# Expert tiles taken one at a time or two at a time on TensorE, in a convolution, attention and mixture-of-experts block

## The reference, cut to what matters

```python
def _L1_ffn_ref(x, router_w, w1, w2, w3):
    flat = x.reshape(-1, C)
    probs = softmax(flat @ router_w.T, axis=-1)
    topk_probs, topk_idx = jax.lax.top_k(probs, TOP_K)
    topk_probs = topk_probs / (sum(topk_probs) + 1e-09)
    gates = jnp.einsum('nk,nke->ne', topk_probs, onehot)
    h1 = jnp.einsum('nc,ehc->neh', flat, w1)
    h3 = jnp.einsum('nc,ehc->neh', flat, w3)
    h = jax.nn.silu(h1) * h3
    y = jnp.einsum('neh,ech->nec', h, w2)
    out = jnp.einsum('ne,nec->nc', gates, y)
```

## Time and profile before

| what | value |
|---|---|
| median of 3 runs | 802.6 us (799.39 to 805.01) |
| the profiled execution, its own time | 802.19 us |
| its span, first to last instruction | 800.4 us |
| mean granted TensorE clock | 0.851 of 2.4 GHz |
| TensorE matmul busy | 650.6 us, 81% of the span |
| the expert tiles, first ups to last scatter landed | 427.4 us to about 780.7 us |

### The profile page before, as it was taken

How to read it: one execution, slowest core, us unless ns; L and a number is a source line. 1 busy time by engine, 2 the same in 40 slices (tenths; PEclk the granted TensorE clock), 3 DMA queues, 4 the chain that set the end, 5 groups by cost and what they waited for, 6 DMA issues and landing times.

```text
span 800.4 us, 13968 instructions
## 1 busy us (share of the span) xinstructions
PE 650.6 (81%) x4632; PEld 487.2 (61%) x4632; DVE 463.2 (58%) x1094; ACT 353.7 (44%) x693; POOL 371.8 (46%) x377
## 2 busy tenths in 40 slices
PE   2597989797979797866206999999999999999960
PEld 2475858585857576664104777677777777777740
DVE  2356677686868676643502566655555665555545
ACT  1143646373727273533203555455555445555520
POOL 2204241767676768727670343334444333444440
PEclk9667868797978788575656999999999999999995
DMA  2000000010101010101173455555556455554608
GB/s 85 0 14 1 14 1 14 19 49 17 51 18 38 18 38 17 51 5 53 50 182 86 148 161 160 165 161 162 179 161 167 152 168 168 179 156 150 191 8 314
DMA packets 46615, 75.47 MB, mean 94 GB/s; under 512 B 7488, under 2 KB 30048, under 8 KB 46544
## 3 DMA queue, kind: packets, MB, share of 16 engines
q1 hardware_dynamic: 34512, 57.12, 24.5%
q0 software_dynamic: 8640, 12.74, 4.8%
q10 hardware_dynamic: 3392, 4.73, 1.8%
HBM read 58.54 MB, written 16.47 MB: 94 GB/s over the span
## 4 chain that ended last, share of the span: by engine, by line
PE 49%; POOL 23%; issue 17%; DVE 6%; DMA 3%; ACT 1%; POOLq 0%; SPq 0%; ACTq 0%; DVEq 0%
PE bk L757 25%; POOL expert_rows L497 15%; PE bk L768 12%; PE bk L745 3%; POOL rr L452 3%; PE bk L775 2%; POOL r L463 1%; PE bk L554 1%; POOL r L458 1%; POOL x2t L481 1%; DMA out<-hid 1%; DMA srow<-expert_results 1%; PE bk L642 1%; POOL grstd L441 1%; PE bk L616 1%
## 5 line engine op out<-in xcount | busy, mean ns | idle before, releaser
L1266 DVE TENSOR_TENSOR units<-bk,silu 128x512 f32<-128x512 f32 x213 | 147.3, 692 | 165.7 <-ACT silu L943 165.7
L519 POOL DMA_INDIRECT expert_results<-yout,xin x142 | 139.5, 983 | 218.3 <-DVE yout L1277 191.5
L757 PE MATMUL bk<-xs,wbuf 64*128 64x256 f32 x1704 | 205.5, 388 | 1.1 <-ACT xs L930 1.1
L757 PEld LDWEIGHTS bk<-xs,wbuf 64*128 64x128 f32 x1704 | 160.8, 189 | 44.4 <-issue 26.6
L943 ACT ACTIVATE silu<-bk 128x512 f32<-128x512 f32 x213 | 127.2, 597 | 87.2 <-PE bk L757 87.2
L497 POOL DMA_INDIRECT expert_rows<-srow,pos x128 | 132.4, 1034 | 44.2 <-issue 37.9
L768 PE MATMUL bk<-units,wbuf 128*64 128x256 f32 x852 | 107.6, 388 | 0.0
L768 PEld LDWEIGHTS bk<-units,wbuf 128*64 128x64 f32 x852 | 54.8, 136 | 32.4 <-issue 11.7
L935 ACT ACTIVATE ysb<-bk 128x256 f32<-128x256 f32 x71 | 27.2, 383 | 84.3 <-PE bk L768 84.3
L452 POOL TENSOR_TENSOR rr<-vare,c_mhalf 128x16 f32<-128x16 f32 x8 | 23.4, 2923 | 74.6 <-DVE vare L1046 74.6
L745 PE MATMUL bk<-const,xin 128*128 128x128 f32 x142 | 31.3, 302 | 29.2 <-DMA xin<-expert_rows 29.2
(11 more groups left out here) (184 smaller groups left out, 963.2 us busy)
## 6 DMA issues: line engine op xcount, KB each, us to landing
wbuf<-in_weights SPq DMA_DIRECT2D x71, 576.0 KB, 4.1
xin<-expert_rows SPq DMA_DIRECT2D x71, 130.0 KB, 2.4
expert_results<-yout,xin POOLq DMA_INDIRECT x142, 2.8
xg<-in_x SPq DMA_DIRECT2D x8, 256.0 KB, 2.8
expert_rows<-srow,pos POOLq DMA_INDIRECT x128, 2.4
srow<-expert_results SPq DMA_DIRECT2D x8, 256.0 KB, 5.1
srow<-expert_results ACTq DMA_DIRECT2D x8, 256.0 KB, 5.9
out<-hid ACTq DMA_DIRECT2D x8, 256.0 KB, 5.2
```

Source lines behind the costliest of these rows:

```text
L519: g.indirect_dma_start(results[:, :], bass.IndirectOffsetOnAxis(ap=xin[:, t % X_SLOTS, h, ROW - 1:ROW].bitcast(U32), axis=0), yout[:, t % ...
L757: last = mm(bank[:, ch * MT:(ch + 1) * MT], wbuf[part, t % W_SLOTS, at:at + P], xs[part, t % 2, :], start=True, stop=True)
L1266: tt(units[:, t % 2, q, :], h3_ps[q], silu[:, q, :], ALU.mult).then_inc(unit_ready, 1)
```

## The change

Tiles are taken in pairs (0, 1), (2, 3), ...; the last pair has one tile. On PE the order becomes: the six up groups of both tiles of pair i, the four row turns of pair i+1, the four result turns of pair i-1, then down of both tiles of pair i. To make this possible:

- `xs` holds two tiles side by side, and ACT stores the turned rows of both in one activation of 512 columns.
- The turned results of both tiles go to one bank, `turned_ps`, which is the bank `h3_ps[0]` of the ups; so result turns wait for the product of group 0 of the pair's second tile, and the next pair's ups wait until `gate_out` has read the bank (`yout_ready`).
- `down` of a tile now comes in the same round as its ups and not in the next.
- `gate_out` does a pair with three operations of 256 columns, and raises `yout_ready` once for both tiles.
- ACT stores the results of both tiles after the turned rows.
- POOL's loop is the same but waits for the pair's `yout_ready`. SP's program is unchanged.

```diff
-            for t in range(NT):
-                pool.wait_ge(yout_ready, t + 1)
+                pool.wait_ge(yout_ready, t // 2 + 1)
...
             def turn_rows(t):
                 pe.wait_ge(xin_loaded[t % X_SLOTS], 16 * (t // X_SLOTS + 1))
-                wait(pe, silu_ready, NU * (t - 1) + 1)
+                wait(pe, silu_ready, NU * (t - 1 - t % 2) + 1)
...
             def up(t, q):
                 if q == 0:
-                    pe.wait_ge(xs_ready, t + 1)
+                    pe.wait_ge(xs_ready, t // 2 + 1)
                     pe.wait_ge(w_loaded[t % W_SLOTS], 16 * (t // W_SLOTS + 1))
+                    wait(pe, yout_ready, t // 2 - 1)
                 wait(pe, unit_ready, NU * (t - 1) + q + 1)
...
             def down(t):
-                wait(pe, yout_ready, t - 1)
+                wait(pe, ysb_ready, t - 1)
                 pe.wait_ge(unit_ready, NU * (t + 1))
...
             def turn_results(t):
                 pe.wait_ge(ysb_ready, t + 1)
+                wait(pe, yout_ready, t // 2)
+                wait(pe, unit_ready, NU * min(2 * (t // 2) + 3, NT - 1) + 1)
                 for h in range(2):
-                    last = turn(yt_banks[t % 2][:, MT + h * P:MT + (h + 1) * P], ysb[:, t % 2, h * P:(h + 1) * P], ident)
+                    at = (2 * (t % 2) + h) * P
+                    last = turn(turned_ps[:, at:at + P], ysb[:, t % 2, h * P:(h + 1) * P], ident)
                 last.then_inc(y_turned, 1)
 
-            turn_rows(0)
-            for t in range(NT):
-                for q in range(NU):
-                    up(t, q)
-                if t + 1 < NT:
-                    turn_rows(t + 1)
-                if t > 1:
-                    turn_results(t - 2)
-                if t > 0:
-                    down(t - 1)
-            turn_results(NT - 2)
-            down(NT - 1)
-            turn_results(NT - 1)
+            for t in range(2):
+                turn_rows(t)
+            for i in range(NPAIR):
+                for t in pair(i):
+                    for q in range(NU):
+                        up(t, q)
+                if i + 1 < NPAIR:
+                    for t in pair(i + 1):
+                        turn_rows(t)
+                if i > 0:
+                    for t in pair(i - 1):
+                        turn_results(t)
+                for t in pair(i):
+                    down(t)
+            for t in pair(NPAIR - 1):
+                turn_results(t)
...
+            def store_xs(i):
+                n = len(pair(i))
+                act.wait_ge(xt_turned, 2 * i + n)
+                wait(act, h3_ready, NU * 2 * i)
+                f(xs[:, 0:n * MT], xt_ps[:, 0:n * MT], ACT.Copy).then_inc(xs_ready, 1)
...
+            def gate_out(i):
+                n = len(pair(i))
+                dve.wait_ge(y_turned, 2 * i + n)
...
+                v.tensor_copy(ysum[:, 0:n, :, :], halves[:, :, :, 0, :]).then_inc(ysum_ready, 1)
+                dve.wait_ge(ysum_ready, 2 * i + 1)
+                tt(ysum[:, 0:n, :, :], halves[:, :, :, 1, :], ysum[:, 0:n, :, :], ALU.add).then_inc(ysum_ready, 1)
+                dve.wait_ge(ysum_ready, 2 * i + 2)
+                tt(yout[:, at:at + n, :, :], ysum[:, 0:n, :, :],
+                   xin[:, at:at + n, :, 2 * C].unsqueeze(3).broadcast_to([P, n, 2, C]), ALU.mult).then_inc(yout_ready, 1)
...
+            for i in range(NPAIR):
+                for t in pair(i):
+                    for q in range(NU):
+                        gated(t, q)
+                if i > 0:
+                    gate_out(i - 1)
+            gate_out(NPAIR - 1)
```

More of the change, by code:

```diff
@@ L25 @@
 NT = (2 * T + NE * (MT - 1)) // MT
+NPAIR = (NT + 1) // 2
 ROW = 2 * C + 2
@@ L213, in hybrid_block @@
         wbuf = sb("wbuf", [P, W_SLOTS, CH * P + CH * C])
-        xs = sb("xs", [P, 2, MT])
+        xs = sb("xs", [P, 2 * MT])
         silu = sb("silu", [P, NU, 512])
@@ L247, in hybrid_block @@
         h3_ps = [bk34[:, 1, :], bk5[:, :], bk6]
-        xt_ps = h1_ps[0][:, 0:MT]
-        yt_banks = [bk0, bk7]
+        xt_ps = h1_ps[0]
+        turned_ps = h3_ps[0]
+        y_banks = [bk0, bk7]
         waited = sem("waited")
@@ L742, in turn_rows @@
                 pe.wait_ge(xin_loaded[t % X_SLOTS], 16 * (t // X_SLOTS + 1))
-                wait(pe, silu_ready, NU * (t - 1) + 1)
+                wait(pe, silu_ready, NU * (t - 1 - t % 2) + 1)
                 for h in range(2):
-                    last = turn(xt_ps[:, h * P:(h + 1) * P], xin[:, t % X_SLOTS, h, 0:2 * C], ident)
+                    last = turn(xt_ps[:, (2 * (t % 2) + h) * P:(2 * (t % 2) + h + 1) * P], xin[:, t % X_SLOTS, h, 0:2 * C], ident)
                 last.then_inc(xt_turned, 1)
@@ L757, in up @@
                         last = mm(bank[:, ch * MT:(ch + 1) * MT], wbuf[part, t % W_SLOTS, at:at + P],
-                                  xs[part, t % 2, :], start=True, stop=True)
+                                  xs[part, t % 2 * MT:(t % 2 + 1) * MT], start=True, stop=True)
                         if ch == 1:
@@ L767, in down @@
                         at = W2_AT + (2 * q + ch) * C
-                        last = mm(yt_banks[t % 2][ch * C:(ch + 1) * C, 0:MT], wbuf[:, t % W_SLOTS, at:at + C],
+                        last = mm(y_banks[t % 2][ch * C:(ch + 1) * C, 0:MT], wbuf[:, t % W_SLOTS, at:at + C],
                                   units[:, t % 2, q, ch * MT:(ch + 1) * MT], start=q == 0, stop=q == NU - 1)
@@ L934, in store_results @@
                 wait(act, y_turned, t - 1)
-                f(ysb[:, t % 2, :], yt_banks[t % 2][:, 0:MT], ACT.Copy).then_inc(ysb_ready, 1)
+                f(ysb[:, t % 2, :], y_banks[t % 2][:, 0:MT], ACT.Copy).then_inc(ysb_ready, 1)
             store_xs(0)
-            for t in range(NT):
[L939 to L948, removed]
+            for i in range(NPAIR):
+                for t in pair(i):
+                    for q in range(NU):
+                        n = NU * t + q
+                        act.wait_ge(h1_ready, n + 1)
+                        wait(act, unit_ready, n - NU + 1)
+                        f(silu[:, q, :], h1_ps[q], ACT.Silu).then_inc(silu_ready, 1)
+                if i + 1 < NPAIR:
+                    store_xs(i + 1)
+                for t in pair(i):
+                    store_results(t)
             for b in range(X_SLOTS):
@@ L1266, in gated @@
                 tt(units[:, t % 2, q, :], h3_ps[q], silu[:, q, :], ALU.mult).then_inc(unit_ready, 1)
[L1268 to L1286, removed]
+            def gate_out(i):
+                n = len(pair(i))
+                dve.wait_ge(y_turned, 2 * i + n)
+                for t in pair(i):
+                    dve.wait_ge(xin_loaded[t % X_SLOTS], 16 * (t // X_SLOTS + 1))
+                    wait(dve, y_scattered[t % X_SLOTS], 32 * (t // X_SLOTS))
+                at = 2 * i % X_SLOTS
+                halves = turned_ps[:, 0:2 * n * P].rearrange("p (t h a c) -> p t h a c", t=n, h=2, a=2)
+                v.tensor_copy(ysum[:, 0:n, :, :], halves[:, :, :, 0, :]).then_inc(ysum_ready, 1)
[4 more added lines that the diff above has]
+                   xin[:, at:at + n, :, 2 * C].unsqueeze(3).broadcast_to([P, n, 2, C]), ALU.mult).then_inc(yout_ready, 1)
+            for i in range(NPAIR):
+                for t in pair(i):
+                    for q in range(NU):
+                        gated(t, q)
+                if i > 0:
+                    gate_out(i - 1)
+            gate_out(NPAIR - 1)
             for i in range(NG):
@@ L1297, with pair @@
 DVE_SETUP = 2
+def pair(i):
+    return range(2 * i, min(2 * i + 2, NT))
 def wait(engine, semaphore, value):
```

## The result

The changed kernel takes 807.14 us (median of 14 runs, 803.53 to 811.75); the kernel before took 801.4 us in as many runs on the same chips (799.01 to 805.01). The ratio is 1.0075, 95% interval 1.0052 to 1.0098: slower by 0.8%, which is 5.7 us. The forecast was 802 and a range of 789 to 815, with "within 1%" the likeliest. The time lies in both, but the interval does not touch 1: the change costs a little where I forecast a gain of 0.4 us.

What follows compares the result with a forecast made beforehand. The prediction took PE, gapless in the expert stage, as the bound, with weight loads barely hidden. Terms of -1.0, -1.0, +1.2 and +0.4 gave -0.4 us on 802.19, so 801.8, forecast as 802, range 789 to 815.

Steps and rivals of the forecast that it cites:

- The PE work of a pair: Expert stage on PE: two tiles together take 9.15 us, against 4.82 us per single-tile round before.
- The seams: PE's lost time between kinds of work, 0.49 us a round; a pair shares one set, so it saves 0.49.
- The seam at the middle of the pair: PE passing from first to second tile's ups: taken as 0; if missed, up to 0.1 to 0.2 us a pair.
- The last rival: PE's gap comes at every tile change, so pairs take at least 9.65 us: 803 to 806 us; chance 0.07.
- The loop up to the fourth scatter: From second tile's ups through gate operations and POOL: results after 5.46 us, fourth scatter out after 10.17, landing in 2.5.
- rival B: Fourth scatter meets weights (lands in 3.3 us), second weight load queues (4.9): pairs 10.17 us, 820 us total; chance 0.15.
- From the landing to the row load: SP's queue: rows are issued about 0.74 us after the fourth scatter lands, the weights 1.17 us after that.
- U: The forecast's time origin in a pair: the start of the second tile's ups on PE.
- 6.07: Fixed part, in us, of the pair's period; half of fourth scatter's landing plus weights' landing, 3.55, is added, giving 9.62.
- The ends: Outside the steady pairs: start +1.2 us, last pair's gate operations +0.4, first two pairs with early weights -1.0.
- Rival A: All weight loads hidden by short landings: pairs 9.15 us, -15.6 us in all, 787 us; chance 0.18.
- The sum: Whole kernel: -1.0 (first two pairs), -1.0 (33 pairs at 9.62), +1.2 (start), +0.4 (tail) make -0.4 us.

Runs made afterwards that it cites:

- the first experiment: Changed kernel with the rows of tile t+2 instead of t+3 loaded behind the weights of tile t on SP's queue: 789.92 us, ratio 0.9841.
- the opposite move: Kernel before, one tile a round, with the rows of tile t+4 instead of t+3 behind the weights of tile t: 853.9 us, ratio 1.0636.

## Why the prediction was right or wrong

**The PE work of a pair, right.** 9.15 us forecast, 2.60 + 6.58, in all 9.19, measured where no weights are late. The seams are per change of kind of work, and half of them went. The seam at the middle of the pair was taken at nothing between 0 and 0.2 us: the first weight loads of the two tiles' ups are 2.60 us apart when nothing is late, which is 12 x 0.216, and in the first experiment the last step of one tile's ups begins at 617.49 and the first of the next at 617.70, one step apart. So it costs nothing. The last rival (the seams stay) is refuted by that.

**The loop up to the fourth scatter, right.** Means over the 29 cycles that begin with tiles 7, 9, ... 63 in the changed kernel: from the first weight load of the second tile's ups to the results 5.46 us (forecast 5.46), POOL 0.85 later (0.86), first to fourth scatter 3.92 (3.85), the fourth's landing 2.57 (2.5). Slower rival B wanted 3.3 there, so it did not come true either; only its direction, slower, did.

**From the landing to the row load, wrong, and this is the step that failed.** The forecast said "SP issues rows about 0.74 after the scatter landed". In the mean of those cycles it is 1.09. In 14 cycles it is the forecast 0.74 or 0.75; in the 15 others it is longer, 0.92 to 2.15, and in 14 of these the rows go out 1.13 to 1.15 us behind the weight issue ahead of them, as closely as SP issues at all. Its issues show why, here 615 to 620 us:

```profile
615.76 0.38 SPq L394 DMA_DIRECT2D xin<-expert_rows  x1
616.92 0.35 SPq L388 DMA_DIRECT2D wbuf<-in_weights  x1
618.05 0.38 SPq L394 DMA_DIRECT2D xin<-expert_rows  x1
619.21 0.35 SPq L388 DMA_DIRECT2D wbuf<-in_weights  x1
```

The fourth scatter of that burst was issued at 614.29 and landed after 2.2 us, at 616.5. Its rows could have gone at 617.2. They went at 618.05, because SP was still at the first tile's pair of loads, four issues in a row 1.13 to 1.16 apart. The first of these stood at 615.76 because the second scatter, issued at 611.71, took 3.3 us beside the weights of 609.77 (these took 4.9). I had followed the loop through the fourth scatter alone. There are two paths: fourth scatter, rows, weights; and second scatter, rows, weights, rows, weights. I had worked out the second (U + 7.6 + 2.5 + 1.9 = U + 12.0 for the first tile's weights), with a scatter that landed in 2.5, and two further issues from there are U + 14.3, just below the fourth's U + 14.6. So they were even in my own numbers. The later of two paths that vary, and are even in the mean, is later than either: 0.35 us in the mean of the cycles. The other terms add 0.2: 0.07 each for the fourth's landing and the scatters, 0.09 from the weights' landing to the ups, 0.03 for the weights' issue, less 0.09 for their landing, 4.51 against 4.6. From 19.18 us for two pairs, the sum of the forecast's terms, it is 19.70. (The forecast's 6.07 is 6.04 by its own terms, so its pair should have been 9.59 and not 9.62; over 33 pairs this slip is 1 us, by which the forecast was luckily nearer.)

**Single late events are no longer absorbed.** The kernel before had some 2 us of cover for the weights (issue to use 6.42 us in the mean, landing 4.27). (The forecast had worked out 3.4, with 2.8 for the landing of a second scatter, which takes 3.5 in the mean there.) The pairs have none, so each delay stays in the time. One scatter left 2.96 us after the one ahead of it instead of 1.29, at 721.71, and that cycle took 21.38 us. This is the second scatter of tile 56, and in all ten kernels it leaves 2.95 to 2.96 us after the first. So it is not chance; the kernel before pays nothing for it. What delays POOL there the trace does not tell.

**The ends, right.** Start: +1.38 against +1.2; first two pairs -0.93 against -1.0; tail +0.45 against +0.4. The first two pairs at 9.15 said in small what the kernel could do without the loop.

**Rival A was right on the gain that lay hidden** but wrong on what would free it. With all weights in time it forecast -15.6 us, and the first experiment gave -11.6, with only the order of SP's queue changed. I had weighed A by whether the landings could be short (they were not, and need not be) and not by whether the wait in front of the weights was necessary.

**The sum.** The forecast of 33 pairs at 9.62 would be 317.5 us from tile 4 to tile 70; they took 324.1. With these 6.6 us and the ends' 0.3 more, the forecast of -0.4 becomes +6.5, against +6.8 by the stretches of the two profiled executions and +5.7 by the medians. The forecast of no change hung on a difference of 0.03 us a pair, 9.62 against 9.65, far less than any term of the loop was known to; that the time still lies in the range says little for it. The main cause is shown: the loop binds (an earlier first result gives its 0.40 back 1:1, the weights put behind an earlier scatter bring the pairs to PE's own pace, the opposite move costs the kernel before 6%). That SP's two paths make the 0.35 of it is read from the trace of the changed kernel, and no experiment parted it from the rest.

## What to carry to other kernels

When work is taken in batches, follow every loop that goes out of the engine and comes back (results, scatter, buffer free, load), and count its cover in batches; a batch holds back its first results until its last are done, and a prefetch depth that was ample before may be used up. If two paths of such a loop come out even, take the later of the two with their spread, not one of them; and before you price a wait, ask whether what stands behind it on its queue needs it at all. Here a load of rows that PE does not turn before 8 to 12 us after its issue, about one pair, held back the weights, and one tile's difference in its place was worth some 17 us by the medians.

## What was new about the hardware

- A burst of four scatters 1.29 us apart beside one weight load lands in 3.24, 2.72, 2.41 and 2.57 us in the mean; with two weight loads just ahead of it, in 4.35, 4.62, 3.27 and 2.97. A scatter of the changed kernel with no weight load under way took 2.15 in the median. So most of the price of the large load falls on the first two, and moving a load changes four landings.
- The 256-column operations of VectorE on fp32 cost 0.41 to 0.43 us, where 128 columns cost 0.28 to 0.29 and 512 cost 0.69: one of 256 instead of two of 128 saves 0.14 us of the engine but makes the first result 0.40 us later, and here the second counted.
- In the kernel before, PE's instruction queue waited up to 1.99 us for weights while the array did not stop once in 100 us. Such waits on a queue, invisible in the busy time, are a measure of how much cover is left.
